# One exp per pair of key chunks, over four PSUM banks, in two attention cores

## The reference

```python
# layer 0: latent keys and values, shared by all heads
q = (c_q @ w_qk.T + b_qk)                      # per head, 64 wide
scores = einsum('bhtd,bsd->bhts', q, c_kv) * scale
attn = softmax(scores, axis=-1)
v = c_kv @ wv_u.T + bv_u
y = einsum('bhts,bhsd->bhtd', attn, v) @ w_proj.T + b_proj
...
# layer 1: ordinary heads
scores = einsum('bhqd,bhkd->bhqk', q, k)
out = einsum('bhqk,bhkd->bhqd', softmax(scores), v) @ Wo.T + bo
```

## Time and profile before

| | |
|---|---|
| median of three runs | 18132.76 us (18122.66 to 18152.79) |
| profiled execution | 18132.74 us, span of its slowest core 18131.2 us |
| spans of the eight cores | 18075.2 to 18131.2 us, mean granted TensorE clock 0.724 to 0.728 |
| busy share of the span | PE 58%, ACT 36%, DVE 22%, weight loads 19%, POOL 1% |
| latent core | about 915 to 4975 us of the span |
| second core | about 11523 to 15680 us of the span |

### The profile page before, as it was taken

The page is one execution under the profiler, slowest core; times in us unless marked ns, Lnnn a source line. Parts: engine busy times, 40 slices in busy tenths (PEclk is TensorE's granted clock), DMA queues, the critical chain, the costliest instruction groups (busy, mean ns, idle before and its releaser), DMA issues.

```text
span 18131.2 us, 113247 instructions; the slowest of 8 cores (18075.2 to 18131.2 us)
## 1 busy us (share of the span) xinstructions
PE 10545.0 (58%) x33144; PEld 3511.6 (19%) x33388; DVE 4058.0 (22%) x4966; ACT 6604.6 (36%) x9550; POOL 211.7 (1%) x265
## 2 busy tenths in 40 slices
PE   4477667666741244444444447666666666666665
PEld 1222222222201111111111113221222212122222
DVE  2012222222142233333333330022211222310000
ACT  1265555555601123322222302455555555400111
POOL 0000000000000000000000000000000000000000
PEclk8687777777865566666666667777777777789776
DMA  1200000000013311001111022100000000045332
GB/s 52 68 3 3 3 3 2 3 3 4 0 52 107 104 30 28 10 23 30 30 30 30 13 82 87 45 5 8 8 3 8 8 8 5 9 137 184 89 89 75
DMA packets 668832, 673.51 MB, mean 37 GB/s; under 512 B 440101, under 2 KB 572374, under 8 KB 651806
## 3 DMA queue, kind: packets, MB, share of 16 engines
q1 hardware_dynamic: 371990, 479.55, 8.5%
q10 hardware_dynamic: 279680, 134.24, 2.7%
q0 software_dynamic: 16592, 52.47, 1.1%
HBM read 521.50 MB, written 148.90 MB: 37 GB/s over the span
## 4 chain that ended last, share of the span: by engine, by line
PE 39%; ACT 20%; DVE 15%; DMA 14%; issue 8%; DVEq 2%; ACTq 1%; SPq 1%; another core or an unknown queue 1%; POOLq 0%
ACT e_sb L870 6%; ACT e_sb L644 5%; PE PS L657 4%; PE PS L884 4%; PE PS L633 4%; PE PS L859 3%; DMA cslab<-scr_qw 3%; DVE den_row L675 2%; DVE den_row L902 2%; DMA wch<-F_w 2%; DMA webf<-F_W 2%; PE PS L1391 2%; PE PS L443 2%; DMA woh<-scr_wo 2%; DVE XT L453 2%
## 5 line engine op out<-in xcount | busy, mean ns | idle before, releaser
L644 ACT ACTIVATE e_sb<-PS 128x1024 bf16<-128x1024 f32 x2048 | 2063.1, 1022 | 439.3 <-PE PS L633 383.4
L870 ACT ACTIVATE e_sb<-PS 128x1024 bf16<-128x1024 f32 x2048 | 2037.8, 1022 | 446.2 <-PE PS L859 435.3
L657 PE MATMUL PS<-e_sb,v 128*65 128x512 bf16 x4096 | 1328.3, 408 | 366.5 <-ACT e_sb L644 310.6
L884 PE MATMUL PS<-e_sb,ckv_tok 128*65 128x512 bf16 x4096 | 1302.9, 401 | 341.4 <-ACT e_sb L870 331.2
L633 PE MATMUL PS<-qaug,kaug 65*128 65x512 bf16 x4096 | 1361.1, 420 | 45.5 <-ACT qaug L618 45.5
L859 PE MATMUL PS<-qaug,ckvT 65*128 65x512 bf16 x4096 | 1339.8, 414 | 45.5 <-ACT qaug L844 45.5
L902 DVE RECIPROCAL den_row<-den_row 1x1024 f32<-1x1024 f32 x64 | 418.6, 6541 | 2808.3 <-ACT den_row L899 2808.3
L675 DVE RECIPROCAL den_row<-den_row 1x1024 f32<-1x1024 f32 x64 | 418.6, 6541 | 2775.9 <-ACT den_row L672 2775.9
L1391 PE MATMUL PS<-XT,cslab 128*128 128x512 bf16 x2000 | 550.9, 432 | 324.3 <-DMA cslab<-scr_qw 315.6
L443 PE MATMUL PS<-y_pair,wtp 128*128 128x512 bf16 x992 | 580.9, 586 | 235.4 <-DVE XT L453 161.9
L453 DVE TENSOR_TENSOR XT<-XT,PS 128x512 f32<-128x512 f32 x896 | 577.2, 686 | 143.7 <-PE PS L443 104.9
(11 more groups left out here) (338 smaller groups left out, 11359.8 us busy)
## 6 DMA issues: line engine op xcount, KB each, us to landing
wch<-F_w SPq DMA_DIRECT2D x64, 512.0 KB, 3.4
wch<-F_w SPq DMA_DIRECT2D x16, 2048.0 KB, 7.9
cslab<-scr_qw POOLq DMA_DIRECT2D x128, 256.0 KB, 3.6
cslab<-scr_qw ACTq DMA_DIRECT2D x128, 256.0 KB, 3.2
webf<-F_W SPq DMA_DIRECT2D x32, 1024.0 KB, 5.3
webf<-F_W ACTq DMA_DIRECT2D x32, 1024.0 KB, 5.4
webf<-F_W SPq DMA_DIRECT2D x64, 512.0 KB, 3.4
webf<-F_W ACTq DMA_DIRECT2D x64, 512.0 KB, 3.8
```

Of the source, the lines that this page charges most:

```text
L644: ss.inc(s_.activation(e_sb[sc % 2][:, :], bank(sb_, 2).rearrange("p a t -> p (a t)"), AF.Exp))
L657: ins = t_.matmul(PS[0:65, pb + half, :], v4[:, sc, h % 2, 0:65], e_sb[sc % 2][:, half * 512:(half + 1) * 512], start=(sc == 0), stop=(sc ...
L870: ss.inc(s_.activation(e_sb[sc % 2][:, :], bank(sb_, 2).rearrange("p a t -> p (a t)"), AF.Exp))
L884: ins = t_.matmul(PS[0:65, pb + half, :], ckv_tok[:, sc, 0:65], e_sb[sc % 2][:, half * 512:(half + 1) * 512], start=(sc == 0), stop=(sc == ...
```

## The change

The same edit in both cores. The two `e_sb` tiles become 2048 columns wide. One exp, `emit_exp2(k)`, takes chunks 2k and 2k+1 together, from banks 0 to 3. It waits for the scores of both chunks and for the PV matmuls that last read its `e_sb` tile (`pvd`). The scores of an even chunk wait for the exp of the pair before, or across windows for the last exp of the window before (`exp_prev`); those of an odd chunk have no wait of their own. The PV matmuls of a chunk wait for the exp of its pair. TensorE's order becomes the scores of a pair, then the PV of the pair before. The core of the diff, for the second attention; the latent one has the same lines with its own operands:

```diff
-            e_sb = [ph.enter_context(sbt(f"e_sb{i}", [128, 1024], BF16))
+            e_sb = [ph.enter_context(sbt(f"e_sb{i}", [128, 2048], BF16))
...
-            exp_done = {0: 0, 2: 0}
+            exp_prev = [0]
+            pvd = {0: 0, 1: 0}
...
                     def emit_qk(sc):
                         sb_ = (sc % 2) * 2
-                        t_.wait_ge(ss.h, exp_done[sb_])
+                        if sc % 2 == 0:
+                            t_.wait_ge(ss.h, exd.get(sc // 2 - 1, exp_prev[0]))
...
-                    def emit_exp(sc):
-                        sb_ = (sc % 2) * 2
-                        s_.wait_ge(stt.h, qk_done[sc])
-                        ss.inc(s_.activation(e_sb[sc % 2][:, :],
-                                             bank(sb_, 2).rearrange("p a t -> p (a t)"),
+                    def emit_exp2(k):
+                        s_.wait_ge(stt.h, qk_done[2 * k + 1])
+                        s_.wait_ge(stt.h, pvd[k % 2])
+                        ss.inc(s_.activation(e_sb[k % 2][:, :],
+                                             bank(0, 4).rearrange("p a t -> p (a t)"),
                                              AF.Exp))
-                        exp_done[sb_] = ss.n
-                        ex_done[sc] = ss.n
+                        exd[k] = ss.n
...
                     def emit_pv(sc):
-                        t_.wait_ge(ss.h, ex_done[sc])
+                        t_.wait_ge(ss.h, exd[sc // 2])
...
+                        k2 = sc // 2
+                        off = (sc % 2) * 1024
                         for half in range(2):
                             ins = t_.matmul(PS[0:65, pb + half, :],
                                             v4[:, sc, h % 2, 0:65],
-                                            e_sb[sc % 2][:, half * 512:(half + 1) * 512],
+                                            e_sb[k2 % 2][:, off + half * 512:
+                                                         off + (half + 1) * 512],
                                             start=(sc == 0), stop=(sc == NC_ - 1))
                         stt.inc(ins)
+                        pvd[k2 % 2] = stt.n
...
                     emit_qk(0)
-                    emit_exp(0)
-                    for sc in range(1, NC_):
-                        emit_qk(sc)
-                        emit_exp(sc)
-                        emit_pv(sc - 1)
+                    emit_qk(1)
+                    emit_exp2(0)
+                    for k in range(1, NC_ // 2):
+                        emit_qk(2 * k)
+                        emit_qk(2 * k + 1)
+                        emit_exp2(k)
+                        emit_pv(2 * k - 2)
+                        emit_pv(2 * k - 1)
+                    emit_pv(NC_ - 2)
                     emit_pv(NC_ - 1)
+                    exp_prev[0] = exd[NC_ // 2 - 1]
```

More of the change, by code:

```diff
@@ L658, in emit_pv @@
                                             v4[:, sc, h % 2, 0:65],
-                                            e_sb[sc % 2][:, half * 512:(half + 1) * 512],
+                                            e_sb[k2 % 2][:, off + half * 512:
+                                                         off + (half + 1) * 512],
                                             start=(sc == 0), stop=(sc == NC_ - 1))
                         stt.inc(ins)
-                    qk_done, ex_done = {}, {}
+                        pvd[k2 % 2] = stt.n
+                    qk_done, exd = {}, {}
                     emit_qk(0)
-                    emit_exp(0)
-                    for sc in range(1, NC_):
-                        emit_qk(sc)
-                        emit_exp(sc)
-                        emit_pv(sc - 1)
+                    emit_qk(1)
[7 more added lines that the diff above has]
+                    emit_pv(NC_ - 2)
                     emit_pv(NC_ - 1)
+                    exp_prev[0] = exd[NC_ // 2 - 1]
                     s_.wait_ge(stt.h, stt.n)
@@ L803, in mla_attn @@
                      for i in range(2)]
-            e_sb = [ph3.enter_context(sbt(f"e0_sb{i}", [128, 1024], BF16))
+            e_sb = [ph3.enter_context(sbt(f"e0_sb{i}", [128, 2048], BF16))
                     for i in range(2)]
```

## The result

| | before | after |
|---|---|---|
| median | 18131.18 us (8 runs, 18112.33 to 18215.76) | 21342.71 us (8 runs, 21316.4 to 21354.28) |
| ratio | | 1.1763, 95% interval 1.1746 to 1.1781 |
| profiled execution | 18132.74 us, span 18131.2 | 21321.32 us, span 21319.8 |

The change makes the kernel 17.6% slower. The forecast of 21030 us was 1.5% low, with the right sign and inside its range of 20000 to 21450.

The account below looks back on a forecast made before the run. No engine at its limit: the attention cores' TensorE-ScalarE ring with two score buffers sets the end. All pairs at half clock add 3251 us, full-clock places return 352: 18132.7 + 2899 = 21030 us; 20800 to 21384 at 0.66, outer range 20000 to 21450.

Parts of the forecast that it names:

- The exps: Both attention cores: 4096 exps of 1024 columns become 2048 of 2048, at 1.87 us each, bounds 1.84 and 1.90.
- The merge: Exps: one merged exp gains 0.07 us per pair against two back to back, 143 us if nothing else moved.
- The score buffers: Banks 0 to 3: score matmuls and exp can no longer overlap, as no second set of banks is left.
- The ring: Attention loops, one pair's round from exp to exp: 3.19 us at full clock against 2.29, 4.05 at half against 3.42.
- The second wait of the exp: Before each exp: the wait for e_sb is always met but is its own instruction; scores to exp take 0.15 us.
- PV under the exp: Attention loops: four PV matmuls, 0.86 us at full clock or 1.71 at half, end inside the exp and cost nothing.
- The clock: TensorE in the attention stretches: most pairs at half clock, granted clock 0.55 to 0.6 instead of 0.77.
- one fifth of the places: 16 places per window (rings and the tail): one fifth, 3.2 places, run at full clock.
- 352 us: Attention windows: 3.2 places at full clock give back 352 us, at 110 us per place over 128 windows.
- The rival in which the clock never comes back: Attention cores: every pair at half clock, +3251 us, 21384 us; chance near never a rise 0.2.
- the hole of 0.6 us: Each half-clock pair: TensorE idles 4.05 - 3.42 = 0.63 us, so what raised the clock is gone.
- Once up, it stays: Attention loops: a clock once at full likely stays, with TensorE busy 1.72 of 3.19 us per ring.

Follow-up runs that it names:

- e1: Changed kernel with each exp of 2048 columns cut back into two of 1024, all waits kept: 21509.08 us, one run.
- e3: Changed kernel with score matmuls padded by zeros from 65 to 128 rows, same instruction count, length and order: 19923.78 us, one run.
- e2: Changed kernel with exps of 1024 and waits by chunk as before the change, TensorE's order by pairs kept: 17777.12 us, one run.
- e5: Changed kernel with one unused matmul behind each pair's PV matmuls: 19966.63 us, one run.
- e4: Changed kernel with two unused matmuls behind each pair's PV matmuls: 20047.61 us, one run.

## Why the prediction was right, and where not

- *The exps.* 1.874 us predicted from 596 and 1022 ns; 1878 ns measured. The merge was put at 143 us; e1 gives 166, its rings 123. Right.
- *The score buffers.* The ring was predicted at 4.05 us at half clock and 3.19 at full; the traces show 4.04 and, in e3, 3.20 (1993.09 to 1996.29). The second wait of the exp, read off another stage, stands in the chain above: from the end of the scores at 2003.20 to the exp at 2003.34 are 0.14 us. Shown from both sides: with the merge undone the loss stays (e1), with the waits undone it turns into a gain (e2).
- *PV under the exp.* Free as said: the chain has no PV in it, and L897 waits 37.8 us in all, for 64 exps, the last of each window.
- *The clock.* Expected at half in most of the loop; it is at half in nearly all of it. The granted clock of the latent core is 0.52, where 0.55 to 0.6 was forecast, so about 4% of its time is at full clock; one fifth of the places was predicted. This is the term of the sum that was mis-sized: 352 us were to be given back, and 18133 + 3251 - 21343 = 41 were. By the starts of the exps, 97 of the 1920 rings of the profiled core are 3.20 us long, which gives back 0.84 x 97 = 81; the other 40 were lost again in places that no run tells apart. The rival in which the clock never comes back (21384 us) is within 0.2% of the result. Which core ends last follows from the same count: the longest, with a span of 21319.8 us, has 97 such rings, the shortest, with 21210.2, has 209.
- *Why the clock stays down.* Here the step itself failed. The prediction held the hole of 0.6 us by itself to be the reason (a timeline prints it as 0.47 of idle, as it draws the last matmul to its end). e3 has that hole and the clock rises in the third ring; e5 leaves 0.2 us of it and the clock rises too. What keeps the clock down here is the hole together with score matmuls that use 65 of 128 rows: take away either, in e3 the rows left idle, in e4 the hole, and it comes back. Before the change the same 65 rows were enough, since the matmuls followed without a hole. So the forecast came near in part by luck: the same reasoning, applied to the merged kernel with 128 rows, expected 21340 us in e3 and missed by 1400. The Trainium skill (TensorE: Matmul & The Clock Gate, A second HAM failure mode: psum-queue depth-cycling) has the micro-idles and the lost clock; the kernel after agrees, though its clock seldom swings and mostly stays down, and e3 shows that the same micro-idles need not cost it.
- *Once up, it stays.* Right where it came up: in 18 of the 128 windows of the profiled core the clock rose inside the loop, and in none of them did it fall back to half before the window's end. Windows view of the kernel after, a window that ran largely at full clock:

```profile
2159.00:2193.00 34.00, 18.18 (x77) 7.24 (x76) 2.37 (x1) 18.39 (x11) 0.00 (x0) 1.00 0.00 0
2193.00:2200.00 7.00, 1.58 (x2) 0.52 (x3) 4.17 (x1) 1.01 (x1) 0.00 (x0) 0.51 0.00 0
```

It holds 1.00 with PE busy 18.18 of 34 us and is back at half (0.51) in the chain behind the window.

So the loss of 21342.71 - 18131.18 = 3211 us parts in two: e3, which has the clock back, still loses 19923.78 - 18131.18 = 1793 us to the ring, and the clock costs the other 1419. As e3 is one run, either may be 50 us off.

The exp alone was not what bounded the loop. At full clock ACT stood idle 0.35 of 2.29 us per pair, and the second score buffer let both engines work at once. The change spent that buffer on a saving of 0.07 us per pair.

## What to carry to other kernels

Before an instruction is merged to save its fixed cost, count the buffers it reads: if the merged one takes all of them, producer and consumer take turns, and the ring is the sum of both. Write the ring down step by step (exp, wait, matmuls, wait) from rows of the trace; it gave both levels here within 0.01 us. If the engine whose instructions you want to merge stands idle between them, look at the order in the queue of the engine that feeds it first: putting the next scores ahead of the PV took 4.5% off this kernel, with one more tile.

## What the runs showed of the hardware

- The clock of TensorE depends on more than whether matmuls run: padding the score matmuls from 65 to 128 rows with zeros, with the same count, length and gaps, moved the granted clock of the latent core from 0.52 to 0.81 and the kernel from 21343 to 19924 us.
- Adding 960 matmuls whose results nobody reads to each attention (e5) made the kernel 1376 us faster, with a clock of 0.77 in the latent core where it was 0.52.
- In e2 some windows of the latent core ran at 0.81, others at 1.00, with all eight cores busy. Windows view of e2, core 1:

```profile
2157.00:2187.00 30.00, 26.45 (x112) 10.52 (x110) 0.33 (x1) 27.58 (x29) 0.00 (x0) 1.00 0.00 1
2213.00:2241.00 28.00, 25.77 (x93) 9.65 (x91) 1.04 (x1) 22.82 (x24) 0.00 (x0) 0.81 0.00 1
```

  At 1.00 it gets through 29 exps in 30 us, at 0.81 through 24 in 28. In the clock records of e2 this level fills 1439 to 1753 us on each of the four cores of one die and is absent on the other four; the medians of the two dies are 17747.5 and 17652.4 us. The Trainium skill (TensorE: Matmul & The Clock Gate, Seeing it yourself) has such a third level, 13/16 of the clock, set for a whole die as a current limit; the trace agrees with the level (0.81) and with the die, and no run here shows what sets it.
